# A gated recurrence on one core: VectorE's loop begins at h's totals, block work behind z's total, narrow closing tiles, 5 r and 3 h tiles ahead of the second half

## The reference

```python
z = sigmoid(xz_t + h @ U_z + vz)
r = sigmoid(xr_t + h @ U_r + vr)
hh = tanh(xh_t + r * h @ U + vh)      # (r * h) @ U
h = (1.0 - z) * h + z * hh
```

## Time and profile before

| | |
|---|---|
| median of 3 runs | 6746.29 us (6745.73 to 6750.2) |
| profiled execution: its own time | 6750.98 us |
| its span | 6748.3 us |
| TensorE busy | 5970.5 us, 88% |
| VectorE busy | 5039.8 us, 75% |
| ScalarE busy | 3502.0 us, 52% |
| mean granted TensorE clock | 0.996 |
| DMA, mean busy share | 0 to 2 tenths |

### The profile page before, as it was taken

The page is one execution under the profiler, slowest core; times in us unless marked ns, Lnnn a source line. Parts: engine busy times, 40 slices in busy tenths (PEclk is TensorE's granted clock), DMA queues, the critical chain, the costliest instruction groups (busy, mean ns, idle before and its releaser), DMA issues.

```text
span 6748.3 us, 483417 instructions
## 1 busy us (share of the span) xinstructions
PE 5970.5 (88%) x200232; PEld 5568.9 (83%) x200232; DVE 5039.8 (75%) x37041; ACT 3502.0 (52%) x23403; POOL 3.9 (0%) x20
## 2 busy tenths in 40 slices
PE   8888888888888888888888888888888888888888
PEld 7888888888888888888888888888888888888887
DVE  5777777777777777777777777777777777777777
ACT  3555555555555555555555555555555555555555
POOL 0000000000000000000000000000000000000000
PEclk8999999999999999999999999999999999999999
DMA  2000000000000000000000000000000000000000
GB/s 82 19 19 16 19 17 19 17 19 16 19 17 19 17 17 17 19 19 16 17 19 19 17 19 16 19 17 19 17 19 16 19 17 19 17 17 19 17 19 17
DMA packets 80315, 129.97 MB, mean 19 GB/s; under 512 B 12336, under 2 KB 18480, under 8 KB 80304
## 3 DMA queue, kind: packets, MB, share of 16 engines
q1 hardware_dynamic: 80304, 129.81, 5.6%
HBM read 20.46 MB, written 8.65 MB: 4 GB/s over the span
## 4 chain that ended last, share of the span: by engine, by line
PE 69%; DVE 27%; issue 3%; ACT 0%; DVEq 0%; SPq 0%; DMA 0%
PE pair_r L280 28%; PE ps_z L280 23%; PE pair_h L280 17%; DVE pair_h L530 8%; DVE h_part L563 5%; DVE h_part L538 5%; DVE h_part L573 3%; DVE h_part L568 3%; DVE keep L564 2%; DVE rh_part L538 0%; DVE rh_part L543 0%; DVE pair_r L530 0%; PE ps_z L238 0%; ACT r_scan L380 0%; DMA u_raw<-in_L_cond_U 0%
## 5 line engine op out<-in xcount | busy, mean ns | idle before, releaser
L280 PEld LDWEIGHTS pair_r<-h_part,u_part 128*128 128x128 f16 x65536 | 1772.7, 96 | 1084.5 <-DVE h_part L538 1080.4
L280 PE MATMUL pair_r<-h_part,u_part 128*128 128x48 f16 x65536 | 1991.5, 183 | 732.7 <-DVE h_part L538 721.2
L280 PE MATMUL pair_h<-rh_part,u_part 128*128 128x48 f16 x65536 | 2000.7, 184 | 19.4
L280 PE MATMUL ps_z<-h_part,u_part 128*128 128x48 f16 x65536 | 1961.9, 183 | 0.0
L280 PEld LDWEIGHTS pair_h<-rh_part,u_part 128*128 128x128 f16 x65536 | 1783.2, 96 | 66.5 <-DVE rh_part L538 27.2
L280 PEld LDWEIGHTS ps_z<-h_part,u_part 128*128 128x128 f16 x65536 | 1782.4, 96 | 0.0
L380 ACT ACTIVATE r_scan<-pair_r 128x4 f32<-128x4 f32 x4096 | 683.5, 176 | 2009.9 <-DVE pair_r L530 1894.8
L530 DVE TENSOR_REDUCE pair_h<-pair_h 128x4 f32<-128x12 f32 x4096 | 722.0, 176 | 698.2 <-PE pair_h L280 698.2
L530 DVE TENSOR_REDUCE pair_r<-pair_r 128x4 f32<-128x20 f32 x4096 | 723.3, 186 | 598.6 <-PE pair_r L280 500.6
L380 ACT ACTIVATE th_z<-ps_z 128x8 f32<-128x8 f32 x2048 | 364.0, 178 | 950.0 <-DVE ps_z L530 950.0
L538 DVE TENSOR_TENSOR_SCAN rh_part<-r_scan,rh_part 128x12 f16<-128x12 f32 x4096 | 748.0, 183 | 140.5
(11 more groups left out here) (72 smaller groups left out, 3034.9 us busy)
## 6 DMA issues: line engine op xcount, KB each, us to landing
w_stage<-w_in SPq DMA_DIRECT2D x384, 256.0 KB, 2.3
x_tok<-in_x SPq DMA_DIRECT2D x68, 128.0 KB, 2.6
out_dram<-o_tok SPq DMA_DIRECT2D x66, 128.0 KB, 2.3
mlp_w<-in_L_cond_W SPq DMA_DIRECT2D x2, 1024.0 KB, 6.8
u_raw<-in_L_cond_U_r SPq DMA_DIRECT2D x1, 1024.0 KB, 5.9
u_raw<-in_L_cond_U_z SPq DMA_DIRECT2D x1, 1024.0 KB, 8.2
u_raw<-in_L_cond_U SPq DMA_DIRECT2D x1, 1024.0 KB, 10.8
w_in<-in_L_cond_W_r SPq DMA_DIRECT2D x4, 256.0 KB, 9.6
```

Of the source, the lines that this page charges most:

```text
L280: last = nc.tensor.matmul(bank[:, SLOT * m:SLOT * m + WIDE].rearrange("p (r a c) -> p r a c", a=n, c=RUN), u_part[:, g, part, k, gm * P:(g ...
```

## The change

TensorE's products are now issued matmul by matmul (`tile`), and the last matmul of each group of products (`closing`) writes 6 instead of 12 columns of each run and, for h, each run once. `ahead` counts single matmuls: 5 for r, 3 for h. VectorE's `step` is cut in two, `gates` (from the r totals through z's total) and `state` (the rest); a pass of the loop holds `state` of one step and `gates` of the next, and the block work follows `gates`. The first `gates` stands ahead of the loop. Behind the last step there is one more set of r and z products and gates, whose results are not used. On ScalarE the r seed of the storing step stands behind `z_mul`.

```diff
--- before.py
+++ after.py
@@ -270,39 +270,42 @@
             pe.wait_ge(s["seed0"], G)
             pe.wait_ge(s["h0_ready"], 1)
 
-            def tile_product(bank, m, g, gm, k, parts, first):
+            def tile(bank, m, g, gm, k, part, parts, first=False, closing=False):
 
                 n = ADDENDS[g] - 1
                 at = k // HC * n * PITCH + k % HC * B * STEP
-                runs = parts[:, at:at + n * PITCH].rearrange("p (a c) -> p a c", c=PITCH)[:, :, 0:RUN]
-                moving = runs.unsqueeze(1).broadcast_to([P, WIDE // (n * RUN), n, RUN])
-                for part in range(PARTS):
-                    last = nc.tensor.matmul(bank[:, SLOT * m:SLOT * m + WIDE].rearrange("p (r a c) -> p r a c", a=n, c=RUN),
-                                            u_part[:, g, part, k, gm * P:(gm + 1) * P], moving,
-                                            start=first and part == 0, stop=False, skip_group_check=True)
-                return last
+
+                repeats, run = (1, B * STEP) if closing else (WIDE // (n * RUN), RUN)
+                runs = parts[:, at:at + n * PITCH].rearrange("p (a c) -> p a c", c=PITCH)[:, :, 0:run]
+                to = bank[:, SLOT * m + WIDE - repeats * n * RUN:SLOT * m + WIDE].rearrange("p (r a c) -> p r a c", a=n, c=RUN)
+                return nc.tensor.matmul(to[:, :, :, 0:run], u_part[:, g, part, k, gm * P:(gm + 1) * P],
+                                        runs.unsqueeze(1).broadcast_to([P, repeats, n, run]),
+                                        start=first, stop=False, skip_group_check=True)
 
             def staggered(banks, g, parts, src, name, t1):
 
 
-                def product(mh, m, k):
-                    return tile_product(banks[mh], m, g, mh * HC + m, k, parts, k == 0 and m == 0)
-
-                first, second = ([(m, k) for m in range(HC) for k in range(kh * HC, (kh + 1) * HC)] for kh in range(2))
-                ahead = 3 if g == R else 2
+                first, second = ([(m, k, part) for m in range(HC) for k in range(kh * HC, (kh + 1) * HC) for part in range(PARTS)]
+                                 for kh in range(2))
+                ahead = 5 if g == R else 3
+
+                def product(mh, tiles, opens=False, closes=False):
+                    for n, (m, k, part) in enumerate(tiles):
+                        last = tile(banks[mh], m, g, mh * HC + m, k, part, parts, opens and n == 0, closes and n == len(tiles) - 1)
+                    return last
 
                 pe.wait_ge(s[src + "0"], t1)
-                for m, k in first:
-                    product(0, m, k)
-                for m, k in first[:ahead]:
-                    product(1, m, k)
+                product(0, first, opens=True)
+                product(1, first[:ahead], opens=True)
                 pe.wait_ge(s[src + "1"], t1)
-                for m, k in second:
-                    last = product(0, m, k)
-                last.then_inc(s[name + "0_mm"], 1)
-                for m, k in first[ahead:] + second:
-                    last = product(1, m, k)
-                last.then_inc(s[name + "1_mm"], 1)
+                product(0, second, closes=True).then_inc(s[name + "0_mm"], 1)
+                product(1, first[ahead:] + second, closes=True).then_inc(s[name + "1_mm"], 1)
+
+            def update_gate():
+                tiles = [(m, k, part) for m in range(K) for k in range(K) for part in range(PARTS)]
+                for n, (m, k, part) in enumerate(tiles):
+                    last = tile(ps_z, m, Z, m, k, part, h_part, n == 0, n == len(tiles) - 1)
+                last.then_inc(s["z_mm"], 1)
 
             def steps(t0, count, proj=None, turn=None):
                 for u in range(count):
@@ -310,10 +313,7 @@
 
 
                     staggered(ps_r, R, h_part, "hs", "r", t1)
-                    for m in range(K):
-                        for k in range(K):
-                            last = tile_product(ps_z, m, Z, m, k, h_part, k == 0 and m == 0)
-                    last.then_inc(s["z_mm"], 1)
+                    update_gate()
 
                     staggered(ps_h, H, rh_part, "rh", "h", t1)
                     if proj is not None:
@@ -343,6 +343,9 @@
                 y_count = pe.snap(n * 2 + 4)
                 with pe.Fori(0, GM) as i:
                     steps(pe.snap(n * TB + i * BODY + TURN), BODY, proj=(pe.snap((n * GM + i + 1) * 16), y_count))
+
+            staggered(ps_r, R, h_part, "hs", "r", T + 1)
+            update_gate()
             put_out(NB + 1)
 
         @block.scalar
@@ -401,10 +404,14 @@
                         store_projection(proj[0], proj[1], 1).then_inc(s["xp_ok"], 1)
                     tanh(th_z[:, :], ps_z, Z, S, "z_sum", t1, "z_th")
 
-                    seed(pair_r, R, nxt)
+                    storing = proj is not None and u % BODY == K
+                    if not storing:
+                        seed(pair_r, R, nxt)
                     act.wait_ge(s["z_th"], t1)
                     A(z_keep[:, :], th_z[:, :], ACT.Copy, scale=-0.5, bias=0.5).then_inc(s["z_keep"], 1)
                     A(z_mul, th_z[:, :], ACT.Copy, scale=H_SCALE / 2, bias=H_SCALE / 2)
+                    if storing:
+                        seed(pair_r, R, nxt)
                     tanh(n_scan[:, half[0], 1], ps_h[0], H, HS, "h0_sum", t1, "h0_th")
                     seed(ps_z, Z, nxt)
                     tanh(n_scan[:, half[1], 1], ps_h[1], H, HS, "h1_sum", t1, "h1_th")
@@ -430,6 +437,8 @@
                           proj=(i, other, act.snap(n * GM + i)))
             act.wait_ge(s["h_ok"], T)
             A(hist[:, :, (T - 1) % (2 * TB)], h_cur, ACT.Copy).then_inc(s["copied"], 1)
+            for hf in range(2):
+                tanh(r_scan[:, half[hf], 1], ps_r[hf], R, HS, f"r{hf}_sum", T + 1, f"r{hf}_th")
             put_out(NB + 1)
 
         @block.vector
@@ -530,13 +539,12 @@
                 return V.tensor_reduce(bank[:, SUM:SUM + m * B].rearrange("p (m b) -> p m b", b=B),
                                        cols(bank, g, 0, m).rearrange("p m a b -> p m b a"), AX_X, ALU.add).then_inc(s[done], 1)
 
-            def step(t1):
-
-
-                def low(parts, count, hi, hf, factors, done):
-
-                    V.tensor_tensor_scan(part_of(parts, count, hf, hi + 1), factors[:, half[hf]].rearrange("p s c -> p (s c)"),
-                                         part_of(parts, count, hf, hi), 0.0, ALU.mult, ALU.subtract).then_inc(s[done], 1)
+            def low(parts, count, hi, hf, factors, done):
+
+                V.tensor_tensor_scan(part_of(parts, count, hf, hi + 1), factors[:, half[hf]].rearrange("p s c -> p (s c)"),
+                                     part_of(parts, count, hf, hi), 0.0, ALU.mult, ALU.subtract).then_inc(s[done], 1)
+
+            def gates(t1):
 
                 def gated_high(hf):
                     dve.wait_ge(s[f"r{hf}_th"], t1)
@@ -556,6 +564,9 @@
                     gated_low(hf)
                 dve.wait_ge(s["z_mm"], t1)
                 total(ps_z, Z, K, "z_sum")
+
+            def state(t1):
+
                 dve.wait_ge(s["h0_mm"], t1)
                 total(ps_h[0], H, HC, "h0_sum")
 
@@ -597,12 +608,14 @@
 
 
                 for u in range(count):
-                    step(dve.snap(t0 + (u + 1)))
+                    state(dve.snap(t0 + (u + 1)))
+                    gates(dve.snap(t0 + (u + 2)))
                     if turn is not None and u < 2:
                         make_out(u, turn[0])
                     if turn is not None and u >= 2:
                         make_y(u - 2, turn[2], turn[1])
 
+            gates(1)
             with dve.Fori(0, NB) as n:
                 other = dve.snap(((n + 1) % 2) * TB)
                 steps(dve.snap(n * TB), TURN, turn=(other, n, dve.snap(n + 2)))
```

## The result

The changed kernel takes 6644.11 us (median of 4 runs, 6643.16 to 6645.04) against 6747.57 for the kernel before on the same chip: a ratio of 0.9846, 95% interval 0.9829 to 0.9863. That is 103 us less. Forecast were 80 less (6667, range 6638 to 6712). Direction, mechanism and most terms came out; one term had the wrong sign.

A forecast was written before the change was run, and what follows sets the result against it. It took a recurrence of 2048 serial steps as the bound, h and z paths ending nearly together. Terms -63 - 25 + 25 - 18 + 1 = -80 gave 6671 us profiled, 6667 as the runs' median; range 6638 to 6712.

The forecast's parts named there:

- the likeliest case: Whole kernel: the forecast from the summed parts, 6667 us, chance 0.66, own range 6645 to 6695.
- three paths: From r, h and z totals to the next r tiles; h and z end within 0.01 us in plain steps.
- Part 1: VectorE's loop begins at h's totals, wait covers the back edge: 0.18 us saved in 352 steps, -63 us.
- Part 2: TensorE's narrow closing tiles: last tile's result 0.010 us sooner, on z's path 0.01 a step; spacing stays 0.025.
- Part 3: 5 r, 3 h tiles ahead: TensorE stalls, 0.015 us carried into z; plain steps by z path, -25 us.
- Part 4: ScalarE, storing step: r seed behind z_mul makes h's tanh later, 3.285 against 3.22 us, +25 us.
- Rival A: ScalarE, storing step: the seed is free and the step goes to 3.17; 6623 us, chance 0.12.
- Part 5: Block work behind z's total on VectorE: turn and first steps 16.07 instead of 16.62 us per block, -18 us.
- 6 (+1): r and z tiles and gates for step T + 1: last output sum behind one more z total, +1 us.
- B: TensorE misses its waits, stall 0.038 instead of 0.015 us, and narrow tiles bring nothing; 6715 us, chance 0.12.
- C: VectorE's back edge costs as much at the h total, 0.73 us from z total; 6744 us, chance 0.05.
- D: TensorE's granted clock falls, over 1.1 us lost per such step; at 100 steps 6777 us, chance 0.05.

The follow-up runs named there:

- loop_alone: Kernel before with only VectorE's new loop place, block work behind z's total and the extra r and z set; 6674.8 us, ratio 0.9893.
- undo_loop: Changed kernel, but VectorE's pass again holds gates and state of one step, block work behind, no extra r and z set; 6699.2 us, ratio 0.9931.
- wide_tiles: Changed kernel with closing matmuls of 48 columns, full size for all tiles; 6665.3 us, ratio 0.9880.
- block_front: Changed kernel with the block work behind the state and ahead of the gates again, new loop place kept; 6651.4 us, ratio 0.9860.
- 20-step version: Changed kernel with 6 r, 3 h matmuls ahead, r seeds behind h's first tanh, and VectorE's loop 3 passes of 20 steps, not 12 of 5; 6945.4 us.
- seed_front: Changed kernel with the storing step's r seed ahead of z_keep again; 6660.1 us, ratio 0.9873.

## Why the prediction was right, and where not

- *The size.* The sum fell 23 us short; the measured 6644 lies 1 us outside the range of the likeliest case (6645 to 6695) and inside the stated one (6638 to 6712). (The sum gives 6666, not 6667.)
- *Reading of the bound.* A recurrence with three paths, the z path close to h's: right. It gave u = 1 to 3 to within 0.003, from two numbers that the chain of waits doesn't name (z_keep behind z tanh, r tile behind z_keep). But in a plain step before, the two paths didn't end within 0.01 of each other: z_keep to r tile took 0.921 to 0.928, where 0.904 is enough (as in the storing step), so the h path was last by about 0.02. The prediction's own terms say so too, 3.19 by z against 3.21. Of the 0.027 that u = 1 gained, 0.010 comes from z's narrow tile and the rest from h's path, which narrow tiles and shorter runs ahead moved out of the way (h's first total at +2.277 instead of +2.347); "shortening the h path alone gives almost nothing" was too strong.
- *Part 1, back edge (-63):* measured -63, u = 0 at 3.215 against 3.21. That is what all parts give together in this step: the loop's new place alone gives 0.169 of it (loop_alone, 3.225), and the other parts would have given 0.057 without the new place (undo_loop). The register work for two step numbers cost nothing.
- *Part 2 (0.010 for z):* right, by wide_tiles.
- *Part 3 (stall of 0.015 in part of the steps):* right in place and kind, the shift was 0.019. The parts to the plain steps make -21 against -25.
- *Part 4 (+25 for the storing step), the step that failed:* measured -4. "The h tanh can't start before z_keep + 0.37": it starts at 0.315. That h's tanh waits for the seed there was right (it comes 0.285 behind its total, 0.212 elsewhere); the wait was priced too high. I had taken the seed's 0.15 from a place where its address stood bare behind an instruction that had just been released, and it was used where another instruction was queued. Another 0.02 lies in "from the h tanh to the r tile is 0.65", which is 0.63 (3413.73 to 3414.36): an activation close behind another is recorded with a later start and a shorter length (0.15 instead of 0.18), so that a start-to-start distance taken from a waiting one is too long. 29 us of difference come from here, more than the whole miss of 23; the plain steps, which gained 4 less than forecast, take a part of it back. Rival A, with 3.17, missed on the other side: the storing step takes 3.213.
- *Part 5 (-18) and 6 (+1):* -17 and +2; block_front gives the block work alone 7 to 9.
- *Rivals.* B's and C's stalls and costs didn't come: z total to h total is 0.56 and not 0.73. D's mechanism is real, as the 20-step version shows: there the clock falls behind pauses of 3.0 to 3.4 between two matmuls. In the steps of the changed kernel, as in those before, the longest such pause is 0.80, and the granted clock stays at 1.00.
- What I didn't weigh is that the changed kernel can be had faster still: 6 and 4 ahead instead of 5 and 3 are worth 17 us, and the order of the seeds with 6 and 3 ahead another 18.

## What to carry to other kernels

In a recurrence, follow every path to the next step's start and write down by how much each is last; a saving counts only up to the second one, and two changes to one step share their gain. Put a loop's back edge where an engine waits for something slow, and count what stands between branch and target. When an instruction moves along its engine's queue, price it at its new place: on ScalarE here, address work was hidden behind an instruction that was already queued and lay bare behind one that had just been waited for.

## What was not expected of the hardware

- A branch back on VectorE takes 0.29 to the next instruction with 103 to some 295 instructions between, and 2.8 to 3.1 with 403 or about 495, with an instruction transfer behind each of the long ones; behind 89 of 95 such pauses TensorE's granted clock was halved for about a step.
- Of two waits ahead of one VectorE instruction, the one written last becomes an instruction of its own; if it is the one that ends last, it costs 0.06.
- A step that ends on the z path makes its successor longer by the stall at TensorE's second wait (0.019), which accounts for about half of seed_front's 16 us (0.020 x 352 = 7).
